# A ring of node rows with 15 places instead of 12, loaded four steps ahead instead of two

## The reference, cut to what matters

```python
edge_index = jnp.stack([src, dst])
x = _layernorm(x + _L0_gnn_ref(x, edge_index, W, attn, W_out))            # 4 heads of 64
x = _layernorm(x + _L1_gnn_ref(x, edge_attr_64, edge_index, ...))         # 4 heads of 32
```

```python
alpha = expa / (asum[dst] + 1e-16)
msg = (v[src] + e) * alpha[..., None]
out = jax.ops.segment_sum(msg, dst, num_segments=n)
out = beta * x_r + (1.0 - beta) * out
return out @ W_m2n.T
```

## Time and profile before

| | us |
|---|---|
| executions, median of 3 | 1313.31 (1311.63 to 1315.16) |
| the profiled execution, span from first to last instruction | 1308.6 |
| TensorE (PE) busy in it | 1172.4 (90%) |
| VectorE (DVE) busy | 1046.9 (80%) |
| ScalarE (ACT) busy | 841.3 (64%) |
| GpSimd (POOL) busy | 840.3 (64%) |

### The profile page before, as it was taken

How to read it: one execution, slowest core, us unless ns; L and a number is a source line. 1 busy time by engine, 2 the same in 40 slices (tenths; PEclk the granted TensorE clock), 3 DMA queues, 4 the chain that set the end, 5 groups by cost and what they waited for, 6 DMA issues and landing times. The chain is left out here.

```text
span 1308.6 us, 28295 instructions
## 1 busy us (share of the span) xinstructions
PE 1172.4 (90%) x6986; PEld 1023.6 (78%) x6986; DVE 1046.9 (80%) x3765; ACT 841.3 (64%) x2783; POOL 840.3 (64%) x1046
## 2 busy tenths in 40 slices
PE   3999999999996799989899599999999993999991
PEld 2888998989995677777777499999999982788880
DVE  3667777777779788889898599999999976788881
ACT  1466666666668765656566466666666675799992
POOL 4888888888854455455454577776777732377775
PEclk9999999999999899999999799999999997999996
DMA  5768888888873488778787777767777732556551
GB/s 150 242 205 268 281 258 265 260 285 258 268 225 122 147 247 241 230 241 252 224 245 219 217 234 217 219 213 231 220 213 216 216 108 91 160 182 191 191 158 55
DMA packets 208937, 277.04 MB, mean 212 GB/s; under 512 B 40060, under 2 KB 140563, under 8 KB 208777
## 3 DMA queue, kind: packets, MB, share of 16 engines
q1 hardware_dynamic: 188793, 224.13, 55.1%
q0 software_dynamic: 19264, 50.85, 13.2%
q10 hardware_dynamic: 720, 0.26, 0.2%
HBM read 159.73 MB, written 117.12 MB: 212 GB/s over the span
## 5 line engine op out<-in xcount | busy, mean ns | idle before, releaser
L744 PE MATMUL banks<-m_ext,node_XT 128*128 128x257 f32 x1568 | 378.8, 385 | 0.0
L744 PEld LDWEIGHTS banks<-m_ext,node_XT 128*128 128x128 f32 x1568 | 287.1, 193 | 33.1
L671 POOL TENSOR_TENSOR node_r<-node_vv,half 128x4 f32<-128x4 f32 (+1 forms) x202 | 211.2, 1045 | 17.2 <-ACT node_X L683 0.2
L702 ACT ACTIVATE node_XT<-banks 128x512 f32<-128x512 f32 x196 | 117.0, 597 | 152.7 <-PE banks L734 149.9
L770 DVE SCALAR_TENSOR_TENSOR node_X<-banks,node_be,node_X 128x256 f32<-128x256 f32 x392 | 169.4, 474 | 56.3 <-ACT node_be L696 55.9
L666 POOL TENSOR_SCALAR node_vv<-node_mv 128x4 f32<-128x4 f32 (+1 forms) x202 | 55.2, 273 | 198.2 <-DVE node_mv L778 171.9
L763 DVE BATCH_NORM_STATS2 node_st<-node_X 128x6 f32<-128x256 f32 x392 | 145.9, 414 | 19.0 <-DMA node_X<-in_x 17.5
L683 ACT ACTIVATE node_X<-node_X,node_r 128x256 f32<-128x256 f32 x326 | 146.1, 496 | 18.9 <-POOL node_r L671 18.8
L709 ACT ACTIVATE node_sq<-node_X 128x256 f32<-128x256 f32 x392 | 157.7, 408 | 0.0
L734 PE MATMUL banks<-ident,node_X 128*128 128x128 f32 x784 | 122.9, 280 | 31.3 <-DVE node_X L784 17.3
L824 POOL DMA_INDIRECT ring<-in_x,src_col x100 | 110.7, 1107 | 37.0 <-POOLq L171 14.3
(11 more groups left out here) (265 smaller groups left out, 2677.7 us busy)
## 6 DMA issues: line engine op xcount, KB each, us to landing
node_X<-in_x SPq DMA_DIRECT2D x196, 256.0 KB, 3.7
out<-node_X SPq DMA_DIRECT2D x196, 256.0 KB, 3.6
ring<-rows SPq DMA_DIRECT2D x210, 128.0 KB, 4.1
rows<-ring SPq DMA_DIRECT2D x100, 256.0 KB, 4.5
rows<-ring SPq DMA_DIRECT2D x200, 128.0 KB, 3.2
MB<-keeps SPq DMA_DIRECT2D x40, 320.0 KB, 4.5
store<-rows SPq DMA_DIRECT2D x90, 128.0 KB, 4.1
MB<-picks SPq DMA_DIRECT2D x50, 128.0 KB, 3.8
```

The source lines that it names most:

```text
L671: pool.tensor_tensor(r[:, s % 4, NT * lo:NT * hi], v, self.c.half[:, NT * lo:NT * hi], ALU.pow).then_inc(self.roots, 1)
L702: act.activation(self.XT[:, n % 2, :], c.psum[:, 4, 0:NT * D], ACT.Copy, bias=1.0).then_inc(self.xt_ready, 1)
L744: last = pe.matmul(ps[:, NT * o + k, 0:D + 1], self.XT[:, o, k * D + h * P:k * D + (h + 1) * P], c.m_ext[:, h, :], start=(h == 0), stop=(h ...
```

## The change

The ring of node rows gets 15 places, and SP issues a load four steps ahead instead of two. The three more places take 6,144 bytes of each partition. The space comes from two tensors:

- The half of `w_qs` that held the skip path's weights goes; no pass reads it. With it go its four of sixteen products in the preparation, its bias load and half the width of the operations on `q`. The unmixed weights of `q` now lie in `Scratch`, which grows, so `FREE` is 71 instead of 72.
- `keep` is no tensor of its own any more. It lies in the ring of edge rows and is made anew in step 4 of each softmax, instead of once in `Masks`.

```diff
-FREE = 72
+FREE = 71
...
-        self.bq_xr = take(P, 2 * DM)
+        self.bq = take(P, DM)
+        self.q = take(P, 2, DM)
...
-LOADS = 16 * (1 + 4 + 6 + 3 + 1 + 3 + 5)
+LOADS = 16 * (1 + 4 + 6 + 3 + 1 + 3 + 4)
...
-                    for bank, pair in ((3, (0, 3)), (4, (1, 2))):
+                    for bank, pair in ((3, (0,)), (4, (1, 2))):
...
-                    pe.matmul(ps[:, 1, 0:2 * DM], w.mean_w, c.w_qs[:, k, :], start=(k == 0), stop=(k == 1))
+                    pe.matmul(ps[:, 1, 0:DM], w.mean_w, w.q[:, k, :], start=(k == 0), stop=(k == 1))
...
-                own(dve.tensor_scalar(c.keep[:, :, :, :], c.cut[:, :, :, :], -1.0, None, ALU.is_ge))
...
-    U = 12
-    AHEAD = 2
+    U = 15
+    AHEAD = 4
...
+            if s == 4:
+                own(dve.tensor_scalar(c.keep[:, :, :, :], c.cut[:, :, :, :], -1.0, None, ALU.is_ge))
...
-        c.w_qs = sb("w_qs", [P, 2, 2 * DM])
+        c.w_qs = sb("w_qs", [P, 2, DM])
...
-        c.keep = sb("keep", [TILES, 2, H, EDGES])
...
+        c.keep = rest[0:TILES, 5 * size + H * P:7 * size + H * P].rearrange("p (k h e) -> p k h e", k=2, h=H)
```

More of the change, by code:

```diff
@@ L202, in _ @@
             with nc.allow_non_contiguous_dma(reason="one bias column"):
-                for out, name in ((w.bq_xr[:, 0:DM], "bq"), (w.bq_xr[:, DM:2 * DM], "bskip"), (w.b_kv[:, 0:DM], "bk"), (w.b_kv[:, DM:2 * DM], "bv")):
+                for out, name in ((w.bq, "bq"), (w.b_kv[:, 0:DM], "bk"), (w.b_kv[:, DM:2 * DM], "bv")):
                     act.dma_start(out, io["L1_gnn_" + name].rearrange("(a d) -> a d", a=1).to_broadcast([P, DM])).then_inc(c.ldd, 16)
@@ L297, in emit @@
                     lhs = w.w_n2m[:, k * P:(k + 1) * P]
-                    for bank, pair in ((3, (0, 3)), (4, (1, 2))):
+                    for bank, pair in ((3, (0,)), (4, (1, 2))):
                         for n, m in enumerate(pair):
-                            pe.matmul(ps[:, bank, (2 * k + n) * DM:(2 * k + n + 1) * DM], lhs, w.w_sqT[:, m, :], start=True, stop=True)
+                            pe.matmul(ps[:, bank, (len(pair) * k + n) * DM:(len(pair) * k + n + 1) * DM], lhs, w.w_sqT[:, m, :], start=True, stop=True)
                 pe.matmul(ps[:, 7, 0:D], w.w_sqT[:, 3, :], w.w_n2m, start=True, stop=True)
@@ L357, in emit @@
                 own(dve.tensor_copy(w.w_skipn, ps[:, 7, 0:D]))
-                own(dve.tensor_copy(c.w_qs[:, :, :].rearrange(both), ps[:, 3, 0:4 * DM]))
+                own(dve.tensor_copy(w.q.rearrange(both), ps[:, 3, 0:2 * DM]))
                 own(dve.tensor_copy(w.kv.rearrange(both), ps[:, 4, 0:4 * DM]))
@@ L372, in emit @@
                 own(dve.scalar_tensor_tensor(out=w.b_ext, in0=w.b_ext, scalar=1.0 / D, in1=ps[:, 0, 0:D + 1], op0=ALU.mult, op1=ALU.subtract))
-                own(dve.scalar_tensor_tensor(out=w.bq_xr, in0=w.bq_xr, scalar=1.0 / D, in1=ps[:, 1, 0:2 * DM], op0=ALU.mult, op1=ALU.subtract))
+                own(dve.scalar_tensor_tensor(out=w.bq, in0=w.bq, scalar=1.0 / D, in1=ps[:, 1, 0:DM], op0=ALU.mult, op1=ALU.subtract))
                 own(dve.scalar_tensor_tensor(out=w.b_kv, in0=w.b_kv, scalar=1.0 / D, in1=ps[:, 2, 0:2 * DM], op0=ALU.mult, op1=ALU.subtract))
@@ L381, in emit @@
                     own(dve.tensor_tensor(w.kv[:, k, :], w.kv[:, k, :], w.b_kv, ALU.add))
-                    own(dve.tensor_tensor(c.w_qs[:, k, :], c.w_qs[:, k, :], w.bq_xr, ALU.add))
+                    own(dve.tensor_tensor(c.w_qs[:, k, :], w.q[:, k, :], w.bq, ALU.add))
                 own.done()
@@ L1387, in emit @@
                 for h in range(2):
-                    last = pe.matmul(ps[:, 7, 0:DM], c.ST[:, o, (2 + h) * P:(3 + h) * P], c.w_qs[:, h, 0:DM], start=(h == 0), stop=(h == 1))
+                    last = pe.matmul(ps[:, 7, 0:DM], c.ST[:, o, (2 + h) * P:(3 + h) * P], c.w_qs[:, h, :], start=(h == 0), stop=(h == 1))
                 last.then_inc(self.q_product, 1)
```

## The result

The changed kernel takes 1292.66 us, the median of four executions (1292.17 to 1295.07), against 1312.47 for the kernel before (1308.76 to 1315.16, four). The ratio is 0.986, with a 95% interval of 0.984 to 0.9881. That is 19.8 us less where 16.8 were predicted. The profiled execution has a span of 1289.9 us, 18.7 less than before.

A forecast was written before the change was run, and what follows sets the result against it. PE was taken to bound score and message, and late node-row loads to slow gather. Gains of 14 + 2.5 + 1.0 less 0.7 made 16.8 us off 1313.3: 1296.5 us, range 1289 to 1309.

The forecast's parts named there:

- Gather: Gather pass: removing DVE's 15.0 us of waits for node rows gains 14 us, between 8.4 and 17.8.
- clean stretches: Five stretches of gather, 100 us in all, without waits for node rows; PE is busy there for 97.1%.
- raw 14.8: Gather's gain in us if PE's work ran at the 97.1% rate, taking 265.2 of 280; lowered to 14.
- The rival in which only the lead grows: SP stays blocked in gather and DVE goes on waiting: 1313 us, chance 0.07.
- crowded masks: Unblocked loads in gather queue ahead of the masks that DVE's scan needs: slower, 1329 us, chance 0.05.
- handshake: In gather, DVE waits for PE instead of loads, and PE for the scan: 1310 us, chance 0.14.
- From gather to message: Stretch between the passes: SP's last row store goes earlier, gaining 2.5 us, between nothing and 5.7.
- The preparation: Start of the kernel: fewer and narrower products against more early node loads, 1.0 us won, between 2.0 lost and 1.4 won.
- five node loads in a row: Preparation: SP issues five instead of three, which could take 2.0 us from the first edge gathers.
- The mask: Softmaxes: one added operation costs 0.66 us in soft1 and nothing in soft2, bounds 0.66 and 1.3.
- Message: Message pass, held to be at PE's limit: no change; more than 3 us would count against the forecast.

The follow-up runs named there:

- lead: Changed kernel with 14 ring places instead of 15, loads still four steps ahead: 1310.29 us, ratio 1.0 to the kernel before.
- tails_first: Changed kernel with POOL's fetch of each tile's last rows moved ahead of the node step before it: 1290.69 us, ratio 0.9836.
- products_back: Changed kernel with the four products of the skip weights put back in the preparation: 1295.34 us, one execution.
- before_swap: Kernel before, with only SP's store issued ahead of its load at each node step: 1295.63 us, ratio 0.9872.
- slack: Changed kernel with 13 ring places and loads two steps ahead, instead of 15 and four: 1292.84 us, ratio 0.9874.

## Why the prediction was right, and which of its steps were not

**Gather** was right in place and size: 13.0 us where I took 14, between bounds of 8.4 and 17.8. PE's rate in the clean stretches, 97.1%, came true: 97.0% between the edges of the pass. The raw 14.8 was too high because that rate was put on the whole window of 280 us, whose edges (440 to 446 and 714 to 720) keep PE busy for only 9.8 of 12 us. On the 268 us between them it gives (248.6 - 0.9) / 0.971 = 255.1, a gain of 12.9. SP's blocking went as said (0.6 us, under 20), DVE's wait for rows too (none, under 2), and no wait for a mask is left. What was off is the cause that I gave. I read DVE's 15.0 us as late loads, and counted two cures, the freed place and 8.5 us more of lead. The lead did nothing (lead: 270.0 us). The step that failed is the reading of the row, which I took as the reason why loads come late. A queue that is blocked at 60 of 66 steps is not late now and then, it is the pace. Read in this way, the gain is the difference between the pace of that chain and of PE, and neither the count of DVE's waits nor their length is in it.

**The rival in which only the lead grows** gave 1313 us, and lead, which does just that, took 1310.29. The rival of the **crowded masks** was a right place with a wrong cause: masks do become the late ones (15.2 us), not when SP is freed but when only the node rows are. The **handshake** did not take the gain back: PE waited 7.5 us for the scan, not 18.7.

**From gather to message** was mis-sized, 2.5 us predicted and 5.1 measured. The step that failed is "the last node store before it is ready when ACT has scaled its rows, at 719.07 + 0.89 = 719.96", 3.2 us after DVE's last rows. I kept that scaling where it stood, and gave its own lateness only "a little more". Once no load was late it ended at 701.21, before DVE's last rows were done (702.06), and the whole lag of 5.7 us went. On POOL 2.3 us of it were given back, which tails_first got; the other links of the chain were quicker in this execution than before. I had named the chain as fixed and not looked at what stands ahead of its fetch on POOL.

**The preparation** was mis-sized, 1.0 predicted and 2.5 measured, over its upper bound of 1.4, and from the wrong row. I counted the products (0.9 us, of which products_back shows nothing) and took the removed bias load for nothing, although it shared its time with SP's longest issues. The loss that I feared from five node loads in a row is not shown: the runs with a lead of two and of four begin soft1 between 388.7 and 390.4, apart from those with the load or with the other order.

**The mask** came as priced: 0.6 us ahead of the tile scan in soft1, where I charged 0.66, and 0.1 in soft2. That the whole stretch of soft1 grew by just 0.7 is in part luck, because before_swap, without that mask, has 54.7 us there too.

**Message** I held to be fixed; it took 1.5 us longer, under the 3 us that would have told against me. Among the other runs without SP's blocking it takes 335.0 to 337.4, with it 334.7 to 335.7. Part of it are waits of DVE for its first rows, 0.4 and 0.5 us in the changed profile; the rest I can't name, and no run was made for it.

The sum is near because two terms were too small (by 1.5 and 2.6 us) and two too favourable (gather by 1.0, message by 1.5).

## What to carry to other kernels

Look at what a DMA queue waits for before asking who waits for its loads. If it waits for its own landed transfers at nearly every step and hardly ever for an engine, suspect that it is the bound; its pace is then at least the time to landing plus what is issued behind it in turn (here 4.1 us of the 4.45 measured). First try another order, so that nothing stands behind a wait for a transfer that has just been issued: here putting the store ahead of the load gave a ratio of 0.9872 with no more places, three more places 0.986 to 0.988. A longer lead did not speed up a queue that was itself the bound; it changed only which load came late, the masks instead of the node rows.

## What the runs showed of the hardware

- A transfer that one engine issues can lengthen the issue of others. One spread load of 64 KB on ACT's queue more, and SP's issue of three weight loads takes 4.26 us together instead of 2.12 (1.53, 2.30 and 0.43 instead of 0.43, 0.64 and 1.05).
- With the queue unblocked, node loads take longer to land: in gather 4.0 us in the median after against 3.5 before, at 251 instead of 238 GB/s, while the stores take 3.7 in both. In slack, with two steps of lead, they take 3.8, and DVE does not wait for node rows there.
